# Axial-attention kernel: context export split straight from PSUM, and Yh's split passes placed only behind evictions of outputs

## What is computed

```python
qkv = einsum('bcxy,oc->boxy', img, w_qkv)            # 8 heads of 64 channels: q, k, v
k = softmax(k, axis=-1)                              # over all 4096 pixels
context = einsum('ndm,nem->nde', k, v)               # 64x64 per head
content_out = einsum('nde,ndm->nem', context, q)
Sx = einsum('ndxy,xid->nixy', q4, Px)
Yh = einsum('nixy,neiy->nexy', Sx, v4)
Yh = batch_norm(Yh)                                  # statistics over all images and heads
Sy = einsum('ndxy,yid->nixy', q4, Py)
rel_pos_out = einsum('nixy,nexi->nexy', Sy, Yh)
out = x + einsum('bcxy,oc->boxy', content_out + rel_pos_out, w_out) + b_out
```

## Time and profile before

| | |
|---|---|
| median of 3 runs | 2961.77 us (2953.87 to 2968.76) |
| the profiled execution | 2955.94 us |
| its span, first to last instruction | 2954.2 us |
| busy: PE, DVE, ACT, POOL | 2606.3, 2057.1, 1699.0, 1415.4 us |
| mean granted TensorE clock | 0.956 |

### The profile page before, as it was taken

One profiled execution on the slowest core, in us unless ns is written; L12 is line 12 of the kernel. 1 busy time (PEld: TensorE's weight loads), 2 busy tenths in 40 slices (PEclk: granted clock), 3 DMA queues, 4 the chain that ended last, 5 costly groups with the idle time before them and its releaser, 6 DMA issues. The chain is left out here.

```text
span 2954.2 us, 119623 instructions
## 1 busy us (share of the span) xinstructions
PE 2606.3 (88%) x54900; PEld 2108.5 (71%) x54900; DVE 2057.1 (70%) x3094; ACT 1699.0 (58%) x2980; POOL 1415.4 (48%) x621
## 2 busy tenths in 40 slices
PE   1999998988998998998988998589899898989997
PEld 1778777777777777777777876466676767766674
DVE  5577677667667677667667665686777768677773
ACT  1565565565565565565556565466665656666563
POOL 2244244244244244244235242686767668576761
PEclk9999999999999999999999999699999999999999
DMA  2242442442343352442344343567767776777763
GB/s 96 74 124 67 113 115 67 123 105 67 96 122 76 98 130 67 106 121 67 95 110 113 92 109 91 132 178 211 182 190 205 189 206 175 214 189 199 188 167 108
DMA packets 448615, 382.35 MB, mean 129 GB/s; under 512 B 307312, under 2 KB 374128, under 8 KB 448112
## 3 DMA queue, kind: packets, MB, share of 16 engines
q1 hardware_dynamic: 429680, 341.14, 45.4%
q10 hardware_dynamic: 18432, 33.56, 3.1%
HBM read 205.79 MB, written 168.82 MB: 127 GB/s over the span
## 5 line engine op out<-in xcount | busy, mean ns | idle before, releaser
L808 POOL TENSOR_TENSOR k_f<-k_f,negmax 128x1024 f32<-128x1024 f32 x128 | 302.9, 2395 | 867.3 <-DVE negmax L773 867.3
L444 PE MATMUL bank<-w_hi,x_hi 128*128 128x256 f16 x2048 | 578.5, 282 | 25.3 <-POOL x_lo L792 23.5
L444 PE MATMUL bank<-w_lo,x_hi 128*128 128x256 f16 x2048 | 572.6, 280 | 3.9 <-issue 3.9
L444 PE MATMUL bank<-w_hi,x_lo 128*128 128x256 f16 x2048 | 571.9, 279 | 0.0
L1251 POOL TENSOR_TENSOR x_f<-x_f,ones 128x1024 f32<-128x1024 f32 x127 | 299.8, 2360 | 260.7 <-DMA x_f<-y_scratch 256.1
L718 DVE TENSOR_TENSOR v_lo<-bank,v_hi 128x256 f16<-128x256 f32 x512 | 214.4, 421 | 283.3 <-ACT v_hi L579 281.0
L1203 DVE TENSOR_TENSOR yb_lo<-x_f,yb_hi 64x1024 f16<-64x1024 f32 x192 | 361.5, 1883 | 43.2 <-ACT yb_hi L1117 41.3
L578 ACT ACTIVATE k_f<-bank 128x256 f32<-128x256 f32 x512 | 200.0, 391 | 323.4 <-PE bank L444 322.1
L444 PEld LDWEIGHTS bank<-w_hi,x_hi 128*128 128x128 f16 x2048 | 297.8, 145 | 33.9 <-issue 25.0
L1050 PE MATMUL bank<-q,rc_both 128*64 128x64 f16 x4096 | 270.9, 244 | 42.8 <-DVE sy_lo L1214 20.9
L502 PE MATMUL bank<-q_hi,rr_hi 128*64 128x64 f16 x4096 | 234.9, 203 | 81.2 <-DVE ybn L758 45.7
(11 more groups left out here) (149 smaller groups left out, 8336.8 us busy)
## 6 DMA issues: line engine op xcount, KB each, us to landing
y_scratch<-yst SPq DMA_DIRECT2D x256, 256.0 KB, 4.4
x_f<-y_scratch SPq DMA_DIRECT2D x256, 256.0 KB, 5.8
q<-q_scratch SPq DMA_DIRECT2D x256, 256.0 KB, 4.2
x_f<-x SPq DMA_DIRECT2D x64, 512.0 KB, 5.7
q_scratch<-q_hi SPq DMA_DIRECT2D x128, 256.0 KB
q_scratch<-q_lo SPq DMA_DIRECT2D x128, 256.0 KB
x_res<-x SPq DMA_DIRECT2D x128, 256.0 KB, 4.8
out<-x_res ACTq DMA_DIRECT2D x128, 256.0 KB, 3.8
```

The source lines that it names most:

```text
L444: mm = pe.matmul(outs, lhs[a], rhs[m], start=first and n == 0, stop=last and n == 2, **kw)
L808: pool.tensor_tensor(kk, kk, negmax[:, :].unsqueeze(1).to_broadcast([P, 8, P]), ALU.add).then_inc(shifted, 1)
```

## The change

`context_out`: the factor is multiplied into the reciprocal (128x1); the two diagonal blocks are then scaled out of PSUM straight into the float16 hi part, and two fused passes read PSUM again and write the rest, (bank x scale) - hi. The tile `cst` is gone. The export counts six steps on its semaphore instead of five, and the waits on it follow.

Splits of the next pair's Yh: every piece moves to a later item, all to "ro" items; pieces (3, 0) and (3, 1), which ACT did behind ro 7, now come behind ro 0 and ro 1 of the pair that uses them. The order of the items themselves stays.

```diff
--- before.py
+++ after.py
@@ -271,7 +271,6 @@
             negmax = sb("negmax", [P, P], F32, p1)
             colmax = sb("colmax", [P, 1], F32, p1)
             cden = sb("cden", [P, 1], F32, p1)
-            cst = sb("cst", [P, DK], F32, p1)
             cst_parts = sb("cst_parts", [P, 2, DK], F16, p1)
             bn6 = sb("bn6", [P, CC, 8, 6], F32, p1)
             mv = sb("mv", [P, CC, 2], F32, p1)
@@ -374,7 +373,7 @@
                                  yst[:, i % YST, :, :]).then_inc(y_st[i % YST], 16)
 
                 def store_context(t):
-                    sp.wait_ge(ctx_out, t * 5 + 6)
+                    sp.wait_ge(ctx_out, t * 6 + 7)
                     sp.dma_start(c_dram[t].rearrange("k p e -> p k e"), cst_parts[:, :, :]).then_inc(ctx_st, 16)
 
                 def turn(b, order):
@@ -458,7 +457,7 @@
                     if piece == 0:
                         pe.wait_ge(p_lo_a, t * 2 + 2)
                         pe.wait_ge(p_lo_b, t * 2 + 2)
-                        pe.wait_ge(ctx_out, t * 5 + 1)
+                        pe.wait_ge(ctx_out, t * 6 + 1)
                     for y2 in range(4 * piece, 4 * piece + 4):
                         for k, (a, m) in enumerate(TERMS):
                             mm = pe.matmul(ctx_ps[:, 0:VW], (p_hi, p_lo)[a][:, y2, :],
@@ -612,15 +611,18 @@
                 dve.wait_ge(ctx_done, t + 2)
                 dve.wait_ge(ctx_st, t * 16 + 16)
                 dve.reciprocal(cden[:, :], ctx_ps[:, P:P + 1]).then_inc(ctx_out, 1)
-                dve.wait_ge(ctx_out, t * 5 + 2)
+                dve.wait_ge(ctx_out, t * 6 + 2)
+                dve.tensor_scalar(cden[:, :], cden[:, :], factors[:, 0:1], None, ALU.mult).then_inc(ctx_out, 1)
+                dve.wait_ge(ctx_out, t * 6 + 3)
                 for g in range(2):
                     s = slice(g * 64, g * 64 + 64)
-                    dve.tensor_scalar(cst[s, :], ctx_ps[s, g * 64:g * 64 + 64], cden[s, 0:1], factors[s, 0:1],
-                                      ALU.mult, ALU.mult).then_inc(ctx_out, 1)
-                dve.wait_ge(ctx_out, t * 5 + 4)
-                dve.tensor_copy(cst_parts[:, 0, :], cst[:, :]).then_inc(ctx_out, 1)
-                dve.wait_ge(ctx_out, t * 5 + 5)
-                dve.tensor_tensor(cst_parts[:, 1, :], cst[:, :], cst_parts[:, 0, :], ALU.subtract).then_inc(ctx_out, 1)
+                    dve.tensor_scalar(cst_parts[s, 0, :], ctx_ps[s, g * 64:g * 64 + 64], cden[s, 0:1], None,
+                                      ALU.mult).then_inc(ctx_out, 1)
+                dve.wait_ge(ctx_out, t * 6 + 5)
+                for g in range(2):
+                    s = slice(g * 64, g * 64 + 64)
+                    dve.scalar_tensor_tensor(cst_parts[s, 1, :], ctx_ps[s, g * 64:g * 64 + 64], cden[s, 0:1],
+                                             cst_parts[s, 0, :], ALU.mult, ALU.subtract).then_inc(ctx_out, 1)
 
             @block.vector
             def _(dve):
@@ -895,17 +897,21 @@
         FIRST_SPLITS = {("sy", 5): ((0, 0), (0, 1)), ("sy", 7): ((1, 0), (1, 1)),
                         ("ro", 1): ((2, 0), (2, 1), (3, 0), (3, 1))}
 
-        SPLITS = {("ro", 1): ((0, 0),), ("ro", 2): ((0, 1),), ("ro", 3): ((1, 0),), ("sy", 0): ((1, 1),),
-                  ("ro", 5): ((2, 0),), ("sy", 4): ((2, 1),), ("ro", 7): ((3, 0), (3, 1))}
+        SPLITS = {("ro", 2): ((0, 0),), ("ro", 3): ((0, 1),), ("ro", 4): ((1, 0),), ("ro", 5): ((1, 1),),
+                  ("ro", 6): ((2, 0),), ("ro", 7): ((2, 1),)}
+        LAST_SPLIT = {("ro", 0): ((3, 0),), ("ro", 1): ((3, 1),)}
 
         LO_DVE = 2 * (YC - 1)
 
         def splits(b, order, kind, hp, i):
 
-            out = [(b * HP, 0, c, h) for c, h in FIRST_SPLITS.get((kind, i), ()) if order is first_turn2 and hp == 0]
-            done = hp if kind == "ro" else hp - 1
-            if kind != "pr" and done >= 0 and (order is not final_turn2 or done + 1 < HP):
-                out += [(b * HP + done + 1, done + 1, c, h) for c, h in SPLITS.get((kind, i), ())]
+            out = []
+            if order is first_turn2 and hp == 0:
+                out += [(b * HP, 0, c, h) for c, h in FIRST_SPLITS.get((kind, i), ())]
+            elif kind == "ro":
+                out += [(b * HP + hp, hp, c, h) for c, h in LAST_SPLIT.get((kind, i), ())]
+            if kind == "ro" and (order is not final_turn2 or hp + 1 < HP):
+                out += [(b * HP + hp + 1, (hp + 1) % HP, c, h) for c, h in SPLITS.get((kind, i), ())]
             return out
 
         with ExitStack() as p2, nc.Block() as block:
```

## The result

The changed kernel takes 2927.11 us (median; 2923.16 to 2927.34, without a fourth, disturbed run of 4405.74) against 2964.16 of the kernel before, measured beside it: a ratio of 0.9874, 95% interval 0.9845 to 0.9903. That is 37 us less. The forecast, 2889, was 73 less than the median of the three earlier runs and 75 less than this one, so about half of it came. Even that may be generous: the two profiled executions are 28.6 us apart, and the kernel before, run again on the chips of the experiments, had medians of 2950.8 to 2956.4. The kernel after was not run there.

The account below looks back on a forecast made before the run. PE, busy 88% of the span, was taken as the spine, with two bare pairs per image bound by DVE. 2955.9 - 34 (export) - 36 (splits) + 0.5 = 2886.4 us, put at 2889; range 2846 to 2936.

Parts of the forecast that it names:

- 0.31 + 0.81 us: Context export: the added 128x1 pass at 0.31 us and the two fused PSUM passes at 0.81 us together.
- rival 3: Context export: new SBUF operands still meet POOL, PSUM passes cost +16 us, splits give -16; 2956, no change; chance 0.08.
- I take three quarters: First pass: of PE's 45.7 us of ybn stalls three quarters come back, the rest reappearing as instruction fetch stalls.
- 31 x 1.74 us is what DVE gains: First pass: each of 31 exports lets the ybn pass start 1.74 us sooner, 54 us in all for DVE.
- the term of -34: First pass: the new context export saves 34 us, 1.1 a turn; ends +22 and -54.
- DVE is then never short of work, so 22.4 and two waits of 0.4: Second bare pair: DVE has 22.4 us of evictions and passes plus two 0.4 us waits for ACT, without idling.
- 4.5 us per image: Second pass: the moved splits save 4.5 us in each of 8 images, -36 us; ends nothing and -73.
- About 40 us instead of 69.5: Second pass: the sign that part 2 is right, PE's waits for DVE before the content product at L1074.
- The idle time takes it: no cost: First bare pair: POOL's split_last ends 3 us later, near 2190.7, and POOL's later 3.88 us of idle time absorbs it.
- POOL comes late by itself, so the new gate costs nothing: Second bare pair: POOL is late already, so starting split_last behind ACT's moved piece adds no time.
- Rival 4: Second pass: late split_last gates SP's y loads, PE stands at ro 0; 3016, likelier 2985; chance 0.06.
- Rival 2: Both passes: stalls are handed on, fetch leaves part 1 -12 us, loaded DVE leaves part 2 -16; 2928; chance 0.21.

Follow-up runs that it names:

- gn_128x1: The changed kernel with the group norm's two 128x2 variance passes each done as two 128x1 passes: 2906.90 us, 0.9840 of the kernel before.
- its two shifted forms: gn_128x1 with 32 or 96 extra small products ahead of image 0's group norm: 2920.22 us (0.9892 of the kernel before) and 2953.36 us (0.9999).
- less_y: The changed kernel with Yh's loads from the third pair on cut to a quarter, so work is left out: 0.9847 of the kernel before.
- less_pool: The changed kernel with GpSimd's add in normalising Yh at an eighth of its width from the third pair on: 0.9781 of the kernel before.
- last_early: The changed kernel with the split of pieces (3, 0) and (3, 1) back behind ro 7: 0.9884 of the kernel before.
- less_dve: The changed kernel with half of VectorE's low-half passes of Yh at half width, so work is left out: 0.9824 of the kernel before.
- gn_shift64: gn_128x1 with 32 extra small products (64 TensorE instructions) ahead of image 0's group norm: 2920.22 us, 0.9892 of the kernel before.

## Why the prediction was half right

**Part 1, the export.** Right in mechanism, with three sizes off. The passes were forecast at 0.31 + 0.81 us for what is now 0.25 + 0.63, start to start, and the plain ones came to 0.64 from the 0.76 that was kept for them (they now write fp16 with one scalar; which of the two made them shorter was not tried): an export of 1.71 us where 2.08 was forecast. The SBUF operand of the fused pass did not meet POOL; rival 3 falls. "I take three quarters": the quarter given to fetch was 11.4 us, "issue" rose by 14, and the counts modulo 256 show that fetch was the right name for it. The step that failed is "31 x 1.74 us is what DVE gains": it took each turn's saving to reach PE. In seven of them DVE came sooner to two 128x2 passes which had cost 0.96 and 0.17 us and now cost 0.79 and 2.29, 1.95 us more, 13.7 in all. gn_128x1 shows it. Without that the term of -34 would have been about right: from the kernel before, the first pass of gn_128x1 is 40 us shorter, those of its two shifted forms 30 and 27.

I had the rule for this in hand and read it off one pair of passes only. The rows showed a cast and a subtract that end with POOL's passes, and PSUM passes that don't; L679 is the same case. The Trainium skill, "SBUF — State Buffer", SBUF: two separate sides, says that VectorE and GpSimd share one pair of ports, held by a VectorE operation with two SBUF inputs or in a two-port mode, or by a GpSimd one, for the whole instruction while the other waits. The trace agrees for passes with two SBUF inputs (L623, 226 ns or 2316; L1209, 1.22 us or 2.17) and with its silence on those that read PSUM. For 128x2 against 128x1 on a single SBUF input (2286 ns against 149) it would need the first to run in a two-port mode and the second not to, which no run here shows.

The Trainium skill, "Runtime: NRT & Kernel Launch", Instruction fetch mechanics, has blocks of 256 instructions and calls the cost of crossing one mostly hidden. The count agrees with both (431 packets, 43 stalls in the kernel after), yet those 43 are 88 us of PE's time, and they rose when DVE's stalls went (34 of 69 us before). Whether a crossing stalls depends on the load of the DMA queues (0.8 us against 17 in the second pass with the quarter loads) and on where in the program it falls.

**Part 2, the splits.** The order did what it should: PE's waits at the Sy banks went, and DVE is no longer idle before ro 0. Two steps failed.
- "DVE is then never short of work, so 22.4 and two waits of 0.4". The two pairs took 23.7 and 24.6, with DVE busy for 22.0 of each. Half of DVE's idle time went (28.9 us left of 58.8). The rest stands behind ro 0, where DVE waits for the ACT passes on the next outputs: 2.65 us in the second of these two, where the working had 0.8. I forecast 4.5 us per image; the bare pairs gave 3.25, and the first pair, whose 1.2 us stall did go, took 0.3 more instead of less. The eviction, put at 3.2 us behind the last Sy bank, came 4.6 behind, and PE's stall before the content product did not shrink to 3 us but was 4.9. "About 40 us instead of 69.5" before the content product was 68.8.
- "The idle time takes it: no cost", and of the second bare pair "POOL comes late by itself, so the new gate costs nothing". This looked at two pairs, and not at the third. POOL's work per image and the landing of Yh did not shorten with the pairs in front, so in the last pair its split ends, and SP's gate opens, 15 us behind ro 0 instead of 8. The Yh loads then coincide with the q loads (DMA share 0.80 instead of 0.65). By itself that costs next to nothing (40.5 us a pair). But in five of the seven last pairs PE's next block of instructions fell due in this stretch; there PE stalls for 1.7 to 2.9 us, and the granted clock of the pair is lower (0.93 instead of 1.00 in the pair shown). That is +18.6 us. less_y takes 14.1 of it back, less_pool 15.5, and moving the code alone 11 and 13; last_early shows that moving the split alone does not. Of the 3.2 us between pairs with and without a stall, 2.2 is the stall itself; how the rest divides between clock and refill was not separated.

Rival 4 had this place, SP's gate, but named the wrong pair and price: not PE waiting for Yh at ro 6 (no such wait appears), but PE waiting for its instructions while the queues are crowded. Rival 2's sum, 2928, is the measured time by luck, with its parts at -19 and -10 where it put -12 and -16. Its reason, fetch taking most of part 1, is half of what happened: of the 31 us of ybn stalls that went, 14 came back as "issue". What the forecast had not allowed for was handed on to the group norm in part 1 and to the last pair in part 2.

## What to carry to other kernels

When a pass of VectorE is slow only in its median, set its end beside the ends of GpSimd's passes; if they agree, list every VectorE pass with that signature near it before costing the edit, since the next one inherits the wait. Ask first whether the pass can simply run before GpSimd is released: here that was worth as much as the rewrite. And when one stretch of a cycle gets shorter, look at the stretch behind it for what does not get shorter (here GpSimd's work and the loads), and at what it will then collide with. A control that adds instructions has its own price, to be read before its time is. And when an engine stalls with no releaser, count its records between such stalls before looking for a cause in the program: a fixed distance speaks for instruction fetch, and then a gain of some microseconds may only be the code having moved.

## What the runs showed of the hardware

- A 128x2 fp32 pass on SBUF took 169 ns alone and 2286 in the median beside GpSimd, a 128x1 pass of the same kind 143 to 155 with or without GpSimd at work (32 passes of gn_128x1).
- A VectorE pass with two SBUF inputs, halved in width, took 1488 ns in the mean against 1743 of the full ones in the same kernel (less_dve), where the shortest of each took 689 and 1206: beside GpSimd halving such a pass saved 255 ns, alone 517.
- PE's "issue" stalls of over 0.9 us stand at one count of its records modulo 256, in all sixteen traces, also with 64, 128 or 192 instructions added ahead; the instruction queue moved one 16 KB packet per 256 records (431 in the kernel after, 432 in gn_shift64).
- These stalls, 17 us in the second pass, fell to 0.8 when one stream of loads was cut to a quarter, and stayed at 13 to 19 when the code was moved.
